# An attention and gate kernel: softmax division steps four tiles later, and the third gate tile's load ahead of the last division

## The reference

```python
xn = _layernorm(x)                       # x: 2 x 2048 x 1024
q, k, v = xn @ wq, xn @ wk, xn @ wv      # 32 query heads, 8 key/value heads of 32
scores = einsum(q, k) * SCALE            # causal
attn = softmax(scores)
s = (attn @ v) @ wo
g = silu(xn @ W_base.T + b_base + lora)  # top 2 of 8 experts, rank 16
out = x + s * g
```

## Time and profile before

| | |
|---|---|
| median of three runs | 3378.37 us (3377.36 to 3383.86) |
| the profiled execution's own time | 3379.06 us |
| its span, first to last instruction | 3377.3 us |
| granted TensorE clock, mean | 0.985 of full speed |
| PE busy | 3274.2 us, 97% of the span |
| DVE busy | 1880.5 us, 56% |
| ACT busy | 1439.7 us, 43% |
| POOL busy | 1355.7 us, 40% |
| DMA moved | 494.53 MB |

### The profile page before, as it was taken

One profiled execution on the slowest core, in us unless ns is written; L12 is line 12 of the kernel. 1 busy time (PEld: TensorE's weight loads), 2 busy tenths in 40 slices (PEclk: granted clock), 3 DMA queues, 4 the chain that ended last, 5 costly groups with the idle time before them and its releaser, 6 DMA issues.

```text
span 3377.3 us, 51290 instructions
## 1 busy us (share of the span) xinstructions
PE 3274.2 (97%) x18048; PEld 2195.1 (65%) x18048; DVE 1880.5 (56%) x4622; ACT 1439.7 (43%) x2658; POOL 1355.7 (40%) x549
## 2 busy tenths in 40 slices
PE   6999999799999999999999999999999899999999
PEld 5888888655555555555555555555553688888887
DVE  6333332287777777677777777767773322223333
ACT  3221121046666666566665666666666111111100
POOL 0000000036766766776776676677667000000000
PEclk9999999899999999999999999999999999999999
DMA  6555554345665666656566566656666444445554
GB/s 231 162 156 167 163 174 151 115 98 117 136 139 130 139 133 135 135 126 135 129 136 136 125 143 129 133 131 136 138 154 157 140 151 137 138 153 195 196 191 170
DMA packets 283503, 494.53 MB, mean 146 GB/s; under 512 B 40864, under 2 KB 156576, under 8 KB 263328
## 3 DMA queue, kind: packets, MB, share of 16 engines
q1 hardware_dynamic: 260256, 333.04, 33.0%
q0 software_dynamic: 20736, 151.00, 22.5%
q10 hardware_dynamic: 2304, 7.87, 0.7%
HBM read 205.03 MB, written 134.74 MB: 101 GB/s over the span
## 4 chain that ended last, share of the span: by engine, by line
PE 65%; DMA 6%; DVE 4%; ACT 2%; issue 2%; SPq 1%; POOL 1%; POOLq 0%; ACTq 0%; DVEq 0%
PE o_ps L1295 14%; PE cols_ps L1340 13%; PE rows_ps L1257 12%; PE rows_ps L799 4%; PE rows_ps L800 4%; PE rows_ps L801 4%; PE cols_ps L1313 3%; PE rows_ps L951 3%; PE rows_ps L949 3%; PE rows_ps L950 3%; DVE row_max L1428 2%; DMA l_few<-l_sb 2%; PE cols_ps L1343 1%; DMA l_sb<-scratch_l_inv 1%; DMA scratch_l_inv<-l_few 1%
## 5 line engine op out<-in xcount | busy, mean ns | idle before, releaser
L1223 POOL TENSOR_TENSOR added<-added,probs 128x2048 f32<-128x2048 f32 (+3 forms) x320 | 1169.4, 3654 | 901.8 <-PE o_ps L1295 807.9
L1428 DVE TENSOR_REDUCE row_max<-rows_ps 128x1 f32<-128x512 f32 x1536 | 994.5, 682 | 286.0 <-PE rows_ps L1257 283.2
L1400 ACT ACTIVATE probs<-cols_ps 128x512 f32<-128x512 f32 x1728 | 921.1, 610 | 357.7 <-PE cols_ps L1340 323.7
L1432 DVE CUSTOM_DVE_ANT_0 masked_rows<-rows_ps,tri 128x128 bf16<-128x128 f32 (+3 forms) x1024 | 483.6, 483 | 181.1 <-PE rows_ps L1257 178.2
L1257 PE MATMUL rows_ps<-k_st,q_st 96*128 96x512 f32 (+3 forms) x1536 | 526.9, 371 | 40.4 <-DMA q_st<-scratch_q_hi 17.2
L1340 PE MATMUL cols_ps<-q_st,k_st 97*128 97x512 f32 x1248 | 521.1, 424 | 0.6
L1295 PE MATMUL o_ps<-probs,v_st 128*32 128x512 f32 (+3 forms) x4224 | 441.5, 535 | 0.0
L1340 PE MATMUL cols_ps<-q_st_last,k_st 97*128 97x512 f32 x928 | 381.3, 425 | 5.1 <-ACT dma_added L1400 3.2
L1257 PEld LDWEIGHTS rows_ps<-k_st,q_st 96*128 96x128 f32 x1536 | 296.0, 193 | 136.2 <-DVE row_max L1428 49.2
L1257 PE MATMUL rows_ps<-k_st,q_st_last 96*128 96x512 f32 (+3 forms) x1024 | 366.0, 384 | 2.7 <-DVE row_max L1432 0.2
L1340 PEld LDWEIGHTS cols_ps<-q_st,k_st 97*128 97x128 f32 x1248 | 237.6, 190 | 176.8 <-issue 112.6
(11 more groups left out here) (113 smaller groups left out, 3791.0 us busy)
## 6 DMA issues: line engine op xcount, KB each, us to landing
dma_added<-probs POOLq DMA_DIRECT2D x144, 1024.0 KB, 7.7
q_st<-scratch_q_hi SPq DMA_DIRECT2D x96, 256.0 KB, 5.3
x_sb<-in_x SPq DMA_DIRECT2D x32, 512.0 KB, 4.0
scratch_xt_hi<-xt_hi SPq DMA_DIRECT2D x32, 512.0 KB, 6.0
scratch_xt_lo<-xt_lo SPq DMA_DIRECT2D x32, 512.0 KB, 6.8
scratch_q_hi<-out_hi SPq DMA_DIRECT2D x64, 256.0 KB, 2.5
scratch_q_lo<-out_lo SPq DMA_DIRECT2D x64, 256.0 KB, 2.9
l_sb<-scratch_l_inv SPq DMA_DIRECT2D x256, 64.0 KB, 5.0
```

Source lines behind the costliest of these rows:

```text
L1223: nc.gpsimd.tensor_tensor(total[:, :, q0:CH], total[:, :, q0:CH], probs_of(c, j)[:, :, q0:CH], ALU.add).then_inc(pool_added, 1)
L1400: nc.scalar.activation(probs_of(c, j)[:, :, i * P:(i + 1) * P], cols_ps[cols_slot(AT_T[t])][:, :].rearrange("p (h q) -> p h q", h=NREP), A ...
L1428: nc.vector.tensor_reduce(into, bank[:, :], AX.X, ALU.max).then_inc(rows_free, 1)
L1432: nc.vector.tensor_tensor_reduce(masked_rows[rows_slot(k)][:, 0:keys], bank[:, 0:keys], tri[:, CH - keys:CH], 1.0, MASKED, ALU.add, ALU.ma ...
```

## The change

Two things are changed. In each chunk's division, I, L2 and L3 come four tiles later, N three and L4 seven. Between L2 and L3 of the very last division (the shortened pass behind the last group), SP now stores gate tile 0, waits until PE has finished gate tile 0, and loads gate tile 2; `stores_before_last` starts with the store of tile 1 and the load of tile 3. These three loads and stores are unrolled from the loop; the number of instructions of each kind is otherwise the same.

In tile numbers, before and after: I of chunks 0 to 3 from 40, 66, 108, 21 to 44, 70, 112, 25; L2 from 41, 67, 109, 22 to 45, 71, 113, 26; L3 from 45, 71, 113, 26 to 49, 75, 117, 30; N from 51, 77, 119, 32 to 54, 80, 122, 35; L4 from 53, 79, 121, 34 to 60, 86, 128, 41.

```diff
@@ -591,11 +591,11 @@
     _t = weighed_at(_c + 1, 2) if _c + 1 < CPB else weighed_at(0, 0) + NTG
     event(_t, "Y", _c)
     event(_t + 4, "L1", _c)
-    event(_t + 12, "I", _c)
-    event(_t + 13, "L2", _c)
-    event(_t + 17, "L3", _c)
-    event(_t + 23, "N", _c)
-    event(_t + 25, "L4", _c)
+    event(_t + 16, "I", _c)
+    event(_t + 17, "L2", _c)
+    event(_t + 21, "L3", _c)
+    event(_t + 26, "N", _c)
+    event(_t + 32, "L4", _c)
@@ -700,8 +700,15 @@
+    def store_first(sp):
+        store(sp, Step(0, 0))
+        wait_apart(sp, acc_full, 2, passed)
+        load(sp, 2, 0)
+
     def stores_before_last(sp):
-        with sp.Fori(0, NPAIR - 1) as pair:
+        store(sp, Step(0, 1))
+        load(sp, 3, 1)
+        with sp.Fori(1, NPAIR - 1) as pair:
             for u in range(2):
                 store(sp, Step(pair, u))
                 load(sp, Step(pair, u).lin(1, 2), u)
@@ -1189,6 +1196,9 @@
                         elif kind == "L3":
+                            if n.lin(1) == NG:
+
+                                gate.store_first(sp)
                             wait_apart(sp, l_inv_stored[par], n.lin(32, 16 * (cc // 2 + 1) - 32 * back), passed)
```

More of the change, by code:

```diff
@@ L825, in products @@
                 tile(pe, Step(pair, u))
-    Gate = namedtuple("Gate", "load_bias load stores_before_last last_stores high tanhs lows first_silu silus first_products "
+    Gate = namedtuple("Gate", "load_bias load store_first stores_before_last last_stores high tanhs lows first_silu silus first_products "
                               "products g_stored")
-    return Gate(load_bias, load, stores_before_last, last_stores, high, tanhs, lows, first_silu, silus, first_products,
+    return Gate(load_bias, load, store_first, stores_before_last, last_stores, high, tanhs, lows, first_silu, silus, first_products,
                 products, g_stored)
```

## The result

| | before | changed |
|---|---|---|
| median of the runs taken together | 3380.57 us (3377.36 to 3383.86, 4 runs) | 3334.32 us (3334.05 to 3336.35, 4 runs) |
| profiled execution, own time | 3379.06 | 3334.6 |
| its span | 3377.3 | 3332.8 |
| granted clock, mean | 0.985 | 0.992 |

The ratio is 0.9864 with an interval of 0.9847 to 0.9882. The change makes the kernel faster, by 44.5 us of span; I had said 35.5.

A forecast was written before the change was run, and what follows sets the result against it. PE, busy for 97% of the span, was taken as the bound, losing time to waits and slow clock. 3379.06 - 26.8 (attention periods) - 8.7 (tail) = 3343.6, said as 3343 us; forecast 3338 to 3352 (chance 0.74), wider range 3337 to 3361.

The forecast's parts named there:

- The excess of the waiting periods: Attention periods with waits at chunk 1's reciprocal: their whole excess over clean ones goes, -26.8 us.
- the clean periods: Six attention periods with waits of at most 0.3 us, mean 117.78; further gain only a bound, 14 x 0.2 us.
- 0.25 us of work either way: On DVE, chunk 1's reciprocal moves behind the shift row; its work of 0.25 us stays the same.
- The tail: Gate after the last division: -11.2 for tile 2's wait, +1.5 and +1 for new waits, -8.7 us; bounds -11.2 and -4.
- 1.5 for wait and clock: Gate tile 2: 0.6 us of wait left and some slow clock, together 1.5 us.
- The 1 us at tile 3: Gate tile 3: a new wait of 0 to 5 us from later loads and stores, taken as 1.
- (2): Rival: an equally long wait holds DVE or PE at another tile; 3357 or 3370 us, chance 0.12.
- the term that I had put at 0: POOL: N of chunk 0 may wait about 1 us longer; taken as 0, uncovered 16 us in all.
- (3): Rival: chunk 2's later product delays its store and then chunk 3's queries, making the kernel slower; chance 0.03.
- (4): Rival: the tail gives nothing, as waits of L3 and gate tile 3 eat the gain; 3352 us, chance 0.08.
- (5): Rival: L1's landing gets later by as much as the step; not faster than 3372 us, chance 0.03.

The follow-up runs named there:

- l4_only: Kernel before with only the store of each chunk's result moved, seven tiles later: 3350.65 us against 3379.13, ratio 0.9914.
- recip_early: Kernel before with only the reciprocals moved, four tiles earlier: 3431.13 us against 3381.70, ratio 1.0146.
- recip1_back: Changed kernel with chunk 1's reciprocal put back at tile 66: 3337.04 us; the kernel before on its chip 3379.13, ratio 0.9869.
- recip2_back: Changed kernel with chunk 2's reciprocal put back at tile 108: 3335.00 us, one run; the kernel before on its chip 3378.49.
- tail_only: Changed kernel with the five old division step times, so only the gate's loads and stores moved: 3366.67 us; the kernel before 3379.13, ratio 0.9964.

## Why the prediction was wrong

The signs, the places and the mechanism of the wait were right; two terms of the sum were too small, and the low end of the range, 3337, was 2.7 us above the measured 3334.32.

**The excess of the waiting periods, -26.8.** Right in kind: the waits at chunk 1's reciprocal went, the clock of the periods went to 1.00. I had put L1 at 2.8 us earlier; in the period shown it was 4.7 us earlier from the period's start (43.2 us after it, not 47.9). As I had said, what held L1 up was SP's queue with L4 in it (`l4_only`). Of the 14.1 us of DVE's waits, 0.7 lie in the last group, so 13.4 belong to the periods; no term hangs on it. And the second half of the price is the clock: `recip_early` pays it 13 times.

**The step that failed: the clean periods, taken at 117.78 and left there.** I gave what could still come out of them as a bound of 14 x 0.2 = 2.8 us, read off DVE's wait, and kept it out of the sum. They came down to 117.29, 14 x 0.49 = 6.8 us. The 0.49 has two parts.

The first, 0.29 a period, goes with L4 alone (117.49 in `l4_only`), and it is the wait that was left at chunk 1's reciprocal. The calmest period before has no listed wait there and still takes 117.71. Beside a period of `l4_only` (for each the window of the period, then one row of DVE and one of PE from its timeline; the kernel before first):

```profile
2029.13:2146.84 117.71, 116.38 (x728) 65.45 (x724) 88.31 (x238) 75.40 (x144) 84.60 (x33) 1.00 0.63 136
2082.13 0.25 DVE L1479 RECIPROCAL l_few<-l_few 128x16 f32<-128x16 f32 x1
2082.90 1.49 PE L1295 MATMUL o_ps<-probs,v_st 128*32 128x512 f32 x12
...
2005.24:2122.71 117.47, 116.18 (x728) 65.46 (x724) 88.17 (x238) 75.38 (x144) 84.64 (x33) 1.00 0.63 136
2058.02 0.24 DVE L1479 RECIPROCAL l_few<-l_few 128x16 f32<-128x16 f32 x1
2058.72 1.50 PE L1295 MATMUL o_ps<-probs,v_st 128*32 128x512 f32 x12
```

From the start of its period the reciprocal starts at 53.00 us and at 52.78, and PE's value products behind it at 53.77 and 53.48. Up to there the two run within 0.05 us of each other, so the 0.2 to 0.3 us are lost at this one place.

The second part, 0.20, is what `l4_only` lacks. The prediction had priced the new places of I, L2 and L3 at nothing ("0.25 us of work either way"). The reciprocal of chunk 1 accounts for 0.05 of it (`recip1_back`) and that of chunk 2 for 0.11 (`recip2_back`, one run); the places of the other two reciprocals, of L2, L3 and N weren't tried. The baseline that I called clean was not free of what was to be removed. A sum that took only the difference between periods could not see it.

**The tail, -8.7.** It was -10.7. The rows of the changed kernel that answer to the earlier trace rows, first SP in the timeline, then the chain:

```profile
2604.51 0.32 SPq L1197 DMA_DIRECT2D scratch_l_inv<-l_few  x1
2604.94 0.84 SPq L700 DMA_DIRECT2D scratch_g<-g_g  x2
2605.89 0.39 SPq L693 DMA_DIRECT2D g_t<-scratch_xt_hi  x1
...
2608.76 1.75 SPq L1204 DMA_DIRECT2D l_sb<-scratch_l_inv  x4
2615.26 0.36 SPq L1209 DMA_DIRECT2D scratch_o<-o_sb  x1
2615.73 1.11 SPq L700 DMA_DIRECT2D scratch_g<-g_g  x2
```

```profile
2608.21 4.83 DMA g_t<-scratch_hw_lo
2613.16 0.49 PE rows_ps L806
2614.12 0.23 PE rows_ps L806
```

The step is right: 4.1 to 6.8 us to landing were the bounds, 4.83 it was, and 0.5 us of wait were left, after which PE keeps its pace of 0.23 us. I had 1.5 for wait and clock, so that is 1.0 too much. The 1 us at tile 3 was wrong: L3's four issues took 1.75 us, L4 went out 10.8 us after L2 (7.1 before) and tile 3 was still in time. The wait of 9.8 less the 0.5 that is left, and the 1.4 (7 x 0.2) of slow matmuls behind it, make 10.7, so 2 us more than I had summed and inside my bounds.

The page on DMA cited in the prediction (the Trainium skill, "DMA: Bandwidth & Descriptors", "Queues, rings and completion order") was one reason to look for a wait at tile 3; the trace has none. L3's loads, issued behind the whole tile, did take longer to land, a median of 3.4 us against 2.1 before; that agrees with an order in the ring but doesn't show it. The fit of the Trainium skill, "DMA: Bandwidth & Descriptors" (section "Anatomy of one DMA — SWDGE (gpsimd) path"), made for one transfer that GpSimd issues, gave an estimate of 4.7 us for the tile's load. SP's four took 7.15 (2605.89 to 2613.04), so the trace doesn't agree with the fit used in this way.

**What no step had:** +1.3 us in the first group, where PE ran at 0.52 between 690 and 700 us and before at 1.00, and -1.5 in the last group. Neither follows an edit: over the profiles of all runs the first cut is anywhere from 828.8 to 831.6, the last group 121.7 to 124.5. They nearly cancel, which is luck.

**The rivals.** (2), the wait turns up elsewhere: it didn't; the 5.3 us at the gate's weights lie in the last group and are 2.1 in the second profile of the same kernel. On POOL, N waits 61.8 us in all for L3's landing where it waited 46.9, and PE doesn't feel it: the term that I had put at 0 was 0. (3), chunk 3's queries late: no wait names them. (4) and (5): no. In all: 26.8 + 8.7 forecast; 6.8 more from the clean periods, 2.0 from the tail, 0.2 from the ends make 44.5.

## What to carry to other kernels

Where one engine's queue issues several independent chains in a fixed order, look for a step that waits late (here a store behind a product) in front of a step that others wait for early (here the first transfer of the next chain), and swap them: moving one store was enough for 92% of the gain in attention. Moving the step that waits instead was enough for 90%, so the two don't add. A step that may have to wait is best put where its engine is ahead of the one it feeds: 3.5 us of waiting cost PE 0.9 us at one tile and 2.2 us cost 2.2 four tiles earlier. And when periods are compared, the quickest seen is no floor: ask what is still waiting in it, and put that into the range whole.

## What I had not expected of the hardware

What a slow clock costs after a stop of PE doesn't grow with the stop, and a stop need not bring it on at all. Stops of 2.0 to 2.2 us in the kernel before made a period 4.5 to 4.8 us too long, stops of 2.4 to 5.4 us in `recip_early` 5.0 to 8.5: beyond the stop that is 2.3 to 2.7 in the one and 1.8 to 3.4 in the other. One stop of 1.9 us in the kernel before cost 3.3, only 1.5 beyond itself. In the kernel before two periods with waits of only 0.4 and 0.7 us at the reciprocal were 2.2 and 2.1 us over the clean ones, each with a window of six microseconds in which PE was granted 0.72 of full speed on average, while one with a wait of 0.8 us was 0.6 over and kept its clock.

`tail_only` has the opposite case: a stop as long as the long ones before, and a clock of 1.00 through the whole period, which is 2.1 us over the calmest of that run (117.64), no more than the stop. The window of the period, and PE's row in the timeline:

```profile
1307.61:1427.35 119.74, 116.38 (x729) 65.46 (x724) 88.35 (x238) 75.41 (x144) 84.54 (x33) 1.00 0.62 134
...
1363.12 0.33 PE L1267 MATMUL rows_ps<-k_st,q_st 96*128 96x128 f32 x1 [2.08 <-DVE row_max L1442]
```

So in this kernel a stop of 0.4 us may bring down the clock and one of 2.1 us may not, and I can't say from these traces which it will be.
